# A selective scan: its C products as ScalarE activations of transposed states, its B rows as broadcast transfers, its denominators' product on GpSimd, its decay in PSUM

## The reference, cut to what matters

```
B = val @ W_B;  C = val @ W_C                       # (tokens, 16) each
Delta = softplus((val @ W_delta + base) @ W_tau)    # (tokens, 256)
dA    = Delta[..., None] * A                        # A = -exp(A_log), (256, 16)
A_bar = exp(dA)
B_bar = expm1(dA) / (dA + 1e-6) * Delta[..., None] * B[:, :, None, :]
h = A_bar_t * h + B_bar_t * val_t[..., None]        # over the tokens t of a sequence
y_t = sum over s of h * C_t
out = y * silu(gate) @ W_out + residual
```

## Time and profile before

| | us |
|---|---|
| median of 3 runs | 5838.19 (5834.34 to 5844.44) |
| the profiled execution | 5834.4 |
| its span, first to last instruction | 5832.6 |
| stage of `mamba_scan` in it | 676.5 to 2515.2 |
| DVE busy in that stage | 1780.99 |
| POOL busy in that stage | 1294.33 |
| PE busy in that stage | 866.83 |
| ACT busy in that stage | 579.01 |

### The profile page before, as it was taken

How to read it: one execution, slowest core, us unless ns; L and a number is a source line. 1 busy time by engine, 2 the same in 40 slices (tenths; PEclk the granted TensorE clock), 3 DMA queues, 4 the chain that set the end, 5 groups by cost and what they waited for, 6 DMA issues and landing times. The chain is left out here.

```text
span 5832.6 us, 81721 instructions
## 1 busy us (share of the span) xinstructions
PE 3935.1 (67%) x27689; PEld 2402.9 (41%) x27691; DVE 4362.2 (75%) x5187; ACT 2377.9 (41%) x3602; POOL 2709.9 (46%) x1660
## 2 busy tenths in 40 slices
PE   3986555434444445569769268888898888996395
PEld 2652111111111111146558036555665556664384
DVE  6882799999999999988600468888887888885301
ACT  1213433333333323312212136666676666776221
POOL 0210576776776766722120235556655666540202
PEclk9998755566666655589779589999999999998597
DMA  2000000000000000000135222122222222210254
GB/s 74 0 4 6 0 0 0 0 0 0 0 0 0 0 0 0 0 16 0 60 127 170 85 63 56 43 49 54 55 59 59 51 52 53 46 41 21 90 189 135
DMA packets 218792, 242.09 MB, mean 42 GB/s; under 512 B 61707, under 2 KB 183492, under 8 KB 217088
## 3 DMA queue, kind: packets, MB, share of 16 engines
q1 hardware_dynamic: 205568, 211.02, 13.3%
q0 software_dynamic: 8704, 24.35, 1.2%
q10 hardware_dynamic: 4224, 2.76, 0.2%
HBM read 119.05 MB, written 35.78 MB: 27 GB/s over the span
## 5 line engine op out<-in xcount | busy, mean ns | idle before, releaser
L971 PE MATMUL mix_scan_y<-mix_scan_hc,ident 128*128 128x512 f32 x512 | 477.2, 1087 | 956.0 <-DVE mix_scan_hc L904 956.0
L2092 DVE TENSOR_TENSOR att_b_prob_low<-att_b_prob,att_b_prob_high 128x1024 f16<-128x1024 f32 (+2 forms) x640 | 773.0, 1208 | 191.1 <-ACT att_b_prob_high L2053 161.5
L895 DVE TENSOR_TENSOR_SCAN mix_scan_h<-mix_scan_a_bar,mix_scan_state,mix_scan_dub 128x512 f32<-128x512 f32 x256 | 834.0, 3296 | 0.1
L2119 DVE TENSOR_REDUCE att_b_neg_max<-att_b_peek 128x1 f32<-128x1024 f32 (+1 forms) x748 | 668.4, 907 | 69.3 <-PE att_b_peek L1941 51.0
L2059 ACT ACTIVATE att_b_prob<-att_b_score,att_soft 128x1024 f32<-128x1024 f32 (+2 forms) x640 | 631.1, 986 | 200.2 <-PE att_b_score L1964 129.8
L852 ACT ACTIVATE mix_scan_a_bar<-mix_val,mix_A 128x512 f32 (+1 forms) x256 | 170.7, 714 | 1219.5 <-DVE mix_scan_h L895 1219.5
L971 PEld LDWEIGHTS mix_scan_y<-mix_scan_hc,ident 128*128 128x128 f32 x512 | 149.9, 323 | 1233.5 <-DVE mix_scan_hc L904 1101.7
L2053 ACT CAST att_b_prob_high<-att_b_prob 128x1024 f16<-128x1024 f32 (+2 forms) x640 | 588.0, 919 | 35.3 <-PE att_b_o L1992 17.6
L1988 PE MATMUL att_b_o<-att_b_vh,att_b_prob_high 128*128 128x65 f16 x4352 | 466.2, 196 | 97.6 <-DVE att_b_heads L2110 55.3
L1988 PEld LDWEIGHTS att_b_o<-att_b_vh,att_b_prob_high 128*128 128x128 f16 x4352 | 401.2, 98 | 220.0 <-DVE att_b_prob_low L2092 127.7
L816 POOL TENSOR_TENSOR mix_scan_dub<-mix_u,mix_scan_b_row 128x512 f32<-128x512 f32 x128 | 279.8, 2186 | 412.6 <-ACT mix_scan_b_row L856 412.6
(11 more groups left out here) (336 smaller groups left out, 9927.2 us busy)
## 6 DMA issues: line engine op xcount, KB each, us to landing
...
att_b_crossed<-att_b_raw SPq DMA_DIRECT2D x512, 64.0 KB, 2.0
...
```

Source lines behind the costliest of these rows:

```text
L895: dve.tensor_tensor_scan(cols(hs, 0, m), cols(a_bar, b, m), cols(dub, b, m), state[:, at:at + 1], ALU.mult, ALU.add).then_inc(scanned, 1)
L971: done = pe.matmul(y_ps[m][:, :], ident[:, :], cols(hc, n % 2, m), start=(n == 0), stop=(n == S_N - 1))
L2092: dve.tensor_tensor(prob_low[:, at:at + width], prob[:, at:at + width], prob_high[:, at:at + width], ALU.subtract).then_inc(low_ready, 1)
L2119: last = dve.tensor_reduce(neg_max[:, first + col:first + col + 1], peek_bank(kind, s)[:, base:base + nb * P], AX.X, ALU.max, negate=True)
```

## The change

The C rows no longer exist as rows. `mamba_delta` computes C with the tokens on the partitions (8 matmuls of 16 columns per group) into `CT`; B stays as 16 rows, which are stored to a DRAM tensor `b_rows` at the end of the stage. PE's loop over groups there is written out.

In `mamba_scan`:

- a_bar is written to PSUM (4 of the 8 banks) and read there by DVE.
- SP loads a B row of 512 tokens, broadcast to 128 partitions, for each unit, into two buffers.
- POOL multiplies the denominators; it also multiplies den by du for the next unit, this by tanh, the inverse by the B row, and the two results. ACT stores the two halves of den swapped, so that both halves are one instruction of 1024.
- DVE has per unit one reciprocal, one (a_bar + 1) tanh, and two scans.
- PE transposes the states in 128 by 128 blocks (8 per unit, in two halves through one PSUM bank); ACT multiplies each transposed block pair by C, now one scalar per partition (`take`), while copying it to SBUF; PE adds these by matmuls with the block as weights and the identity as moving operand, which turns them back.
- ACT also saves the state, times carry, and makes the residual (`keep_two`); DVE's addition to X is one instruction per tile. Gating and additions of a group are done during units 1, 3 and 5 of the next one.

The diff, without most of the removed lines (they are in the functions above), the list of semaphores, and the last lines of each engine's part:

```diff
-            BC = ctx.enter_context(nc.sbuf_tensor(name + "_BC", [2 * S_N, TOK], F32))
-            mamba_delta(nc, dram, val, u, BC, A, w_out, name + "_dt")
-            mamba_scan(nc, X, ident, val, gate, u, BC, A, w_out, mean, rstd, name + "_scan")
+            CT = ctx.enter_context(nc.sbuf_tensor(name + "_CT", [P, NT * S_N], F32))
+            b_rows = nc.dram_tensor(name + "_b_rows", (S_N, TOK), F32, kind="Internal").ap()
+            mamba_delta(nc, dram, val, u, CT, b_rows, A, w_out, name + "_dt")
+            mamba_scan(nc, X, ident, val, gate, u, CT, b_rows, A, w_out, mean, rstd, name + "_scan")
...
+            sp.wait_ge(b_ready, NG)
+            sp.dma_start(b_rows, B[:, :]).then_inc(b_stored, 16)
+            sp.wait_ge(b_stored, 16)
...
             pe.wait_ge(w_loaded, LOADS * 16)
-            with pe.Fori(0, NG) as g:
-                pe.wait_ge(u_ready, len(PIECES))
+            pe.wait_ge(u_ready, len(PIECES))
+            for g in range(NG):
                 pe.wait_ge(comb_ready, PRIMED + g)
                 x = [u[:, bass.ds(g * GRP + c * TOK, GRP)] for c in range(KD)]
                 for c in range(KD):
-                    pe.matmul(bc_ps[0:2 * S_N, :], w_bc[:, c * 2 * S_N:(c + 1) * 2 * S_N], x[c],
+                    pe.matmul(b_ps[0:S_N, :], w_bc[:, c * 2 * S_N:c * 2 * S_N + S_N], x[c],
                               start=(c == 0), stop=(c == KD - 1))
+                for j in range(GT):
+                    for c in range(KD):
+                        pe.matmul(ct_ps[:, j * S_N:(j + 1) * S_N], u[:, g * GRP + c * TOK + j * P:g * GRP + c * TOK + (j + 1) * P],
+                                  w_bc[:, c * 2 * S_N + S_N:(c + 1) * 2 * S_N], start=(c == 0), stop=(c == KD - 1))
...
-                    act.copy(BC[:, bass.ds(g * GRP, GRP)], bc_ps[0:2 * S_N, :])
+                    act.copy(B[:, bass.ds(g * GRP, GRP)], b_ps[0:S_N, :]).then_inc(b_ready, 1)
+                    act.copy(CT[:, bass.ds(g * GT * S_N, GT * S_N)], ct_ps[:, 0:GT * S_N])
...
+        tanh, den, factor, dub = (sb(n, [P, AHEAD * W]) for n in ("tanh", "den", "factor", "dub"))
+        b_row, inv = sb("b_row", [P, AHEAD * GRP]), sb("inv", [P, AHEAD * GRP])
+        hs, hcT = sb("h", [P, AHEAD * W]), sb("hcT", [P, AHEAD * W])
         yg = sb("yg", [P, W])
...
+        kept = sb("kept", [P, 2 * D])
...
+        a_bar = [ps(f"a{i}", W) for i in range(AHEAD)]
+        y_ps = [ps("y0"), ps("y1")]
+        hT_ps, out_ps = ps("hT"), ps("out")
...
+        @block.sync
+        def _(sp):
+            sp.wait_ge(set_up, SETS)
+            def body(g, first, last):
+                for n in range(S_N):
+                    b, unit = n % 2, g * S_N + n
+                    wait_apart(sp, row_used, unit + 1, (set_up, SETS))
+                    sp.dma_start(b_row[:, b * GRP:(b + 1) * GRP],
+                                 b_rows[n:n + 1, bass.ds(g * GRP, GRP)].to_broadcast([P, GRP]))\
+                        .then_inc(b_landed[b], 16)
+            turns(sp, body)
...
+            def pair(u, b):
+                wait_apart(pool, den_ready, u + 1, (set_up, SETS))
+                pool.tensor_tensor(inv[:, b * GRP:(b + 1) * GRP], cols(den, b, 0), cols(den, b, 1), ALU.mult)\
+                    .then_inc(pair_ready, 1)
+            def inputs(u, b, g):
+                pool.tensor_tensor(both(cols(factor, b)), both(cols(den, b)),
+                                   du[:, :].rearrange("p (m t) -> p m t", m=KD)[:, :, bass.ds(g * GRP, GRP)], ALU.mult)\
+                    .then_inc(den_used, 1)
+            pair(0, 0)
+            inputs(0, 0, 0)
+            def body(g, first, last):
                 for n in range(S_N):
                     b, unit = n % 2, g * S_N + n
...
+                    more = not (last and n == S_N - 1)
+                    at = g if n + 1 < S_N else g + 1
+                    wait_apart(pool, expm1_ready, unit + 1, (set_up, SETS))
+                    wait_apart(pool, den_used, AHEAD + unit + 1, (set_up, SETS))
+                    pool.tensor_tensor(cols(factor, b), cols(factor, b), cols(tanh, b), ALU.mult).then_inc(tanh_used, 1)
+                    if more:
+                        pair(unit + 1, 1 - b)
+                    wait_apart(pool, inverse_ready, unit + 1, (set_up, SETS))
+                    wait_apart(pool, b_landed[b], (g * (S_N // 2) + n // 2 + 1) * 16, (set_up, SETS))
+                    one = inv[:, b * GRP:(b + 1) * GRP]
+                    pool.tensor_tensor(one, one, b_row[:, b * GRP:(b + 1) * GRP], ALU.mult).then_inc(row_used, 1)
+                    wait_apart(pool, scanned, (unit + 1) * KD, (set_up, SETS))
+                    wait_apart(pool, tanh_used, AHEAD + unit + 1, (set_up, SETS))
+                    wait_apart(pool, row_used, AHEAD + unit + 1, (set_up, SETS))
+                    pool.tensor_tensor(both(cols(dub, b)), both(cols(factor, b)),
+                                       one.unsqueeze(1).to_broadcast([P, KD, GRP]), ALU.mult).then_inc(input_ready, 1)
+                    if more:
+                        inputs(unit + 1, 1 - b, at)
...
+            def take(g, n):
+                b, unit = n % 2, g * S_N + n
+                at = state[:, :].rearrange("p (m s) -> p m s", m=KD)[:, :, n:n + 1]
+                act.activation(at, both(cols(hs, b))[:, :, GRP - 1:GRP], ACT.Identity, scale=carry[:, bass.ds(g, 1)])\
+                    .then_inc(state_saved, 1)
+                for half in range(HALVES):
+                    act.wait_ge(h_turned, unit * HALVES + half + 1)
+                    if half == 0:
+                        wait_unless_first(act, summed, (unit - 1) * HALVES + PRIMED)
+                    for j in range(GT // HALVES):
+                        t = half * (GT // HALVES) + j
+                        last = act.activation(hcT[:, b * W + t * D:b * W + (t + 1) * D], hT_ps[:, j * D:(j + 1) * D],
+                                              ACT.Identity, scale=CT[:, bass.ds((g * GT + t) * S_N + n, 1)])
+                    last.then_inc(hc_ready, 1)
...
+                    wait_apart(act, den_used, unit + 1, (set_up, SETS))
                     for m in range(KD):
-                        act.activation(cols(den, b, m), x[m], ACT.Identity, scale=a(m, A), bias=eps[:, 0:1])
+                        done = act.activation(cols(den, b, 1 - m), x[m], ACT.Identity, scale=a(m, A), bias=eps[:, 0:1])
+                    done.then_inc(den_ready, 1)
+                    wait_apart(act, tanh_used, unit + 1, (set_up, SETS))
                     for m in range(KD):
-                        act.activation(cols(tanh, b, m), x[m], ACT.Tanh, scale=a(m, half_A))
-                    wait_apart(act, scanned, (unit + AHEAD - 1) * KD, (set_up, 1))
+                        done = act.activation(cols(tanh, b, m), x[m], ACT.Tanh, scale=a(m, half_A))
+                    done.then_inc(tanh_ready, 1)
+                    wait_apart(act, scanned, (unit + 1) * KD, (set_up, SETS))
                     for m in range(KD):
-                        done = act.activation(cols(a_bar, b, m), x[m], ACT.Exp, scale=a(m, A))
+                        done = act.activation(a_bar[b][:, m * GRP:(m + 1) * GRP], x[m], ACT.Exp, scale=a(m, A))
                     done.then_inc(bars_ready, 1)
-                    act.wait_ge(b_ready, unit + 1)
-                    act.copy(b_row[:, b * GRP:(b + 1) * GRP], b_ps[b][:, :]).then_inc(b_copied, 1)
+                    if n >= AHEAD:
+                        take(g, n - AHEAD)
+                    elif not first:
+                        take(g - 1, S_N + n - AHEAD)
+                    if n in (3, 5) and not first:
+                        keep_two(g - 1, (n - 3) // 2)
+            def keep_two(g, part):
+                act.wait_ge(added, PRIMED + g * GT + part * 2)
+                for j in range(2):
+                    t = g * GT + part * 2 + j
+                    act.activation(kept[:, j * D:(j + 1) * D], X[:, rows(t)], ACT.Identity,
+                                   scale=keep_scale[:, bass.ds(t, 1)], bias=keep_shift[:, bass.ds(t, 1)])\
+                        .then_inc(kept_ready, 1)
...
+            def factors(u, b):
                 one = inv[:, b * GRP:(b + 1) * GRP]
-                dve.wait_ge(input_ready, unit + AHEAD - 1)
-                dve.tensor_tensor(one, cols(den, b, 0), cols(den, b, 1), ALU.mult).then_inc(pair_ready, 1)
-                dve.scalar_tensor_tensor(out=cols(tanh, b), in0=cols(a_bar, b), scalar=1.0,
-                                         in1=cols(tanh, b), op0=ALU.add, op1=ALU.mult).then_inc(expm1_ready, 1)
-                dve.wait_ge(pair_ready, unit + 1)
+                dve.wait_ge(pair_ready, u + 1)
                 dve.reciprocal(one, one).then_inc(inverse_ready, 1)
...
+                dve.wait_ge(tanh_ready, u + 1)
+                dve.wait_ge(bars_ready, u + 1)
+                dve.scalar_tensor_tensor(out=cols(tanh, b), in0=a_bar[b][:, :], scalar=1.0, in1=cols(tanh, b),
```

(60 more changed lines are left out.)

184 lines of the change are left out of this document (56 added, 128 removed).

## The result

The changed kernel takes 5282.7 us (median of 4 runs, 5278.7 to 5293.9); the kernel before, run beside it, 5838.9. The ratio is 0.905, 95% interval 0.903 to 0.907. The profiled execution took 5278.7 us, its span is 5277.1 (5832.6 before).

The account below looks back on a forecast made before the run. Bound: DVE and POOL excluding each other around one buffer, not arithmetic. From 5834.4 us, 586 saved in the scan stage (127 units of 9.58) and 13 added in mamba_delta give 5261, as median 5265; range 5240 to 5450.

Parts of the forecast that it names:

- The exclusion of DVE and POOL: DVE instructions reading two SBUF tensors and POOL products exclude each other; decay in PSUM saves scans 4.12 us per unit.
- POOL's line: POOL's five products per unit of mamba_scan, the longest line after the change: 9.58 us, bounds 9.34 and 9.94.
- waits for POOL's own last result: Two POOL products per unit wait for POOL's preceding result, 0.12 us each, taking 9.34 to 9.58.
- Ring: Denominators' product, reciprocal, decay+1, factor times tanh between POOL and DVE: 4.8 us against POOL's 5.9, slack 1.1.
- start: Scan stage from the first den to the first factor times tanh: 7.75 us.
- last unit: POOL's products in the last unit of the scan stage: 6.06 us.
- tail: Scans, turns, products by C, sums, gate and additions after POOL's last unit: 16.2 us.
- The wait for the gate: TensorE's first sum of a group waits for DVE's gate; some 1.3 + 2.0 us late per group, taken up.
- Rival (d): B row broadcast through SP's queue is slow: at a landing of 28 us the kernel takes 5909; chance 0.03.
- (a): Scan still excludes POOL, by pointer scalar or its own kind: 295 us more, 5560; chance 0.13.
- (b): ScalarE and TensorE set the unit's time, about 10.5 us on average: 5380; chance 0.12.
- (c): POOL's waits on computed values show, 0.2 us at each of five products, unit 10.6: 5390; chance 0.10.

Follow-up runs that it names:

- the run on collisions: Changed kernel plus three DVE instructions of 512 per unit: scalar_tensor_tensor with PSUM tensor and pointer, tensor_scalar with pointer, tensor_scalar with constant; 5436.0 us in one run.

## Why the prediction was right

**What bounded the kernel.** Right. The exclusion of DVE and POOL hangs on where the decay lies: with the decay in SBUF the 6.58 us return. The forecast bare scans of 2.46 a pair are 2.45. One reading was off by 0.3 us: a bare scan of 1.23 behind the end of L828 (1509.33) ends at 1510.56, not near 1510.3. L830 lasted 0.79 longer than L828, so already there POOL lost less than one bare scan.

**Where the rest of the gain is.** The unit fell by 13.59 - 9.79 = 3.80 us: 2.61 by the decay in PSUM, as undoing it shows. The other 1.2 belong to the rest of the change, and no run divides them. They are the distance to the kernel with the decay back in SBUF, where the exclusion still holds and DVE waits only 1.0 us a unit for POOL (125.9 us in all), less than two products by C of 0.68. So C's move may be part of them. With the decay in PSUM it gives nothing: products in the same form put back on DVE (one tensor in PSUM, 0.679 us each) cost no time. What it gives besides is room, read from the code and not tried: the rows of B and C spread into PSUM took banks which the decay now takes (two buffers of 1024, four of the eight banks).

**POOL's line.** Right as the bound, short by 0.20 us: 9.58 summed, 9.78 measured. Without the waits for POOL's own last result it is 9.43 instead of 9.34, start to start 2.32 and 1.23 instead of 2.30 and 1.22, and each of the two waits costs 0.17 instead of 0.12. The 0.12 came from one pair of rows, L828 to L830, the 2.30 from a difference. 127 x 0.20 = 25 us is the mis-sized term of the sum.

**Ring, start, last unit, tail.** From den to the first factor times tanh 7.76 us, 7.75 summed. L963 is done at 1260.86, 1.73 before L861 needs it; 1.1 was forecast. From the last factor times tanh to the last addition (1958.65) 21.2 us, against 6.06 + 16.2 = 22.3.

**ScalarE and TensorE.** Hidden, as said. The four products take 0.463 each, 0.473 forecast; the line from the decay to the end of tanh is 7.1 us (1263.32 to 1270.37), not 8.4. The four sums between the halves take 1.9 us, about the 2.0 forecast, but the turns and sums overlap at their ends and the second turn takes 0.89 instead of 1.09 (mean granted clock of the stage 0.69): the second half is turned 3.6 us after the scans, not 4.4. The products of that half and den with tanh are 0.3 shorter together. The wait for the gate is there, 51.6 us in 7 places, and POOL waits for nothing behind it.

**B rows.** Transfers of 256 KB in the trace after:

```profile
mix_scan_b_row<-mix_b_rows SPq DMA_DIRECT2D x128, 256.0 KB, 3.2
```

3.2 us, below the lower bound of 4.7; 17.9 were free. Rival (d) had nothing in it.

**mamba_delta.** The mechanism stands: ScalarE waits 1.7 us for comb in every second group, three of the other groups are not quite covered (0.43 us), and moving the small matmuls out of the way saves time in all three traces. They took 1.96 in seven groups and 3.60 in the first, against 1.9 to 4.0. The size can't be told from one trace of each kernel: the first memset of the scan stage comes 8.3 us later than before, where 13 were forecast, and the same code differs by up to 10 us between traces. The set-up, from that memset to the first den, is 1.05 us instead of 2.10, not 0.7 longer: the table load of 1.28 us that stood ahead of the first den now stands behind it. Together that is 7.3 against 13.7. The store of B lands in 3.9 us some 20 us before the stage ends, hidden as said.

**Sum.** 5261 for the profiled execution, 5278.7 measured: +25.3 for the units, -1.1 for the end, -6.4 ahead of the stage. The total is off by only 18 us because errors of opposite sign offset each other in part, and the -6.4 is within what two traces of the same code differ by. That is luck in the size, not in the mechanism.

**The rivals.** (a) fell with the scans of 1.264 us, and with the run on collisions, which shows why L925 misled. (a)'s price was too high as well: where the scans do collide, they cost POOL 0.72 + 0.91 = 1.63 us a unit, not 2.3. (b) fell with ScalarE's products twice. (c) fell too: waits on computed values for other engines cost nothing that the unit shows, and what POOL's waits do cost, 0.35 us a unit, is the term for its own last result that stood in the sum with 0.24. The page "GPSIMD Engine Reference" of the Trainium skill, section "Engine selection", which spoke against the product on POOL, was right in direction, but my price for it, 155 us, was too high: 101 were measured (0.8875 against 0.9049 of 5826), since the product on DVE collides and POOL loses 0.45 of the 1.23 us again.
